# Reordering the two score units of each key tile in a relative-position attention block

## The reference

```
qh, kh, vh = heads of (q @ in_proj_weight.T + in_proj_bias);  qh = qh / sqrt(d)
scores = einsum('bhid,bhjd->bhij', qh, kh)
rel    = clip(pos[None, :] - pos[:, None], -64, 64) + 64
bias   = take_along_axis(einsum('bhid,rd->bhir', qh, rel_pe), rel)
attn   = softmax(scores + bias);  out = einsum('bhij,bhjd->bhid', attn, vh) @ out_w.T + out_b
x = layernorm(x + out)
x = layernorm(x + (gelu(x @ bw1.T + b1) @ bw2.T + b2))     # bw: alpha * sign(w)
```

## Time and profile before

| | |
|---|---|
| median of three runs | 2361.61 us (2361.12 to 2361.84) |
| profiled execution | 2361.56 us, of which the span is 2359.6 us |
| TensorE busy | 2227.5 us (94% of the span) |
| VectorE busy | 1739.1 us (74%) |
| ScalarE busy | 1573.1 us (67%) |
| GpSimd busy | 1085.8 us (46%) |
| mean granted clock of TensorE | 0.978 |

### The profile page before, as it was taken

The page is one execution under the profiler, slowest core; times in us unless marked ns, Lnnn a source line. Parts: engine busy times, 40 slices in busy tenths (PEclk is TensorE's granted clock), DMA queues, the critical chain, the costliest instruction groups (busy, mean ns, idle before and its releaser), DMA issues. The chain is left out here.

```text
span 2359.6 us, 47824 instructions
## 1 busy us (share of the span) xinstructions
PE 2227.5 (94%) x14580; PEld 1261.9 (53%) x14580; DVE 1739.1 (74%) x3447; ACT 1573.1 (67%) x2192; POOL 1085.8 (46%) x1803
## 2 busy tenths in 40 slices
PE   8996899999999999999999999999999998899997
PEld 5563444444444444444444444444444443688886
DVE  4443777777777777777777777777777772788885
ACT  3433377777777777777777777777777776466766
POOL 1001444554445544455445545454554431567663
PEclk9998599999999999999999999999999999899999
DMA  9997777777777777777777677777777752333421
GB/s 305 400 352 265 204 208 202 210 214 211 206 207 208 208 213 209 210 203 208 212 209 212 201 208 215 209 208 202 210 213 209 209 178 73 100 102 111 111 65 45
DMA packets 334570, 468.55 MB, mean 199 GB/s; under 512 B 89797, under 2 KB 262550, under 8 KB 334486
## 3 DMA queue, kind: packets, MB, share of 16 engines
q0 software_dynamic: 120960, 215.78, 33.9%
q1 hardware_dynamic: 204358, 243.32, 32.7%
q10 hardware_dynamic: 9168, 8.52, 1.1%
HBM read 244.73 MB, written 221.25 MB: 197 GB/s over the span
## 5 line engine op out<-in xcount | busy, mean ns | idle before, releaser
L933 ACT ACTIVATE probs<-weigh_ps 128x1024 f32<-128x1024 f32 x1024 | 1048.9, 1025 | 471.8 <-PE weigh_ps L1100 468.0
L985 DVE CUSTOM_DVE_ANT_1 ring_ps<-ring_ps,band_all 128x512 f32<-128x512 f32 x1008 | 681.0, 716 | 263.8 <-PE ring_ps L1061 263.6
L1061 PE MATMUL ring_ps<-keys,queries 48*128 48x512 f32 x2048 | 827.1, 468 | 40.1 <-DVE partial_max L974 14.0
L1100 PE MATMUL weigh_ps<-queries,keys 50*128 50x512 f32 (+3 forms) x2688 | 751.0, 385 | 1.3 <-ACT probs L933 0.6
L974 DVE TENSOR_REDUCE partial_max<-ring_ps 128x2 f32<-128x1024 f32 x512 | 627.7, 1226 | 112.3 <-PE ring_ps L1061 80.8
L1061 PEld LDWEIGHTS ring_ps<-keys,queries 48*128 48x128 f32 x2048 | 370.7, 187 | 524.7 <-issue 398.9
L1117 PE MATMUL sum_ps<-probs,values 128*32 128x512 f32 x4096 | 546.6, 605 | 0.1
L839 POOL COPY carried<-carried 128x252 f32<-128x252 f32 x430 | 159.3, 396 | 568.2 <-ACT carried L922 568.2
L1085 PE MATMUL weigh_ps<-ident,band_all 128*128 128x128 f32 x2048 | 363.2, 290 | 19.3 <-ACT carried L922 16.5
L1100 PEld LDWEIGHTS weigh_ps<-queries,keys 50*128 50x128 f32 x2688 | 356.3, 186 | 14.9 <-ACT probs L933 9.5
L1085 PEld LDWEIGHTS weigh_ps<-ident,band_all 128*128 128x128 f32 x2048 | 213.6, 141 | 249.9 <-ACT probs L933 104.6
(11 more groups left out here) (119 smaller groups left out, 1857.3 us busy)
## 6 DMA issues: line engine op xcount, KB each, us to landing
band_scr<-carried SPq DMA_DIRECT2D x256, 512.0 KB, 4.8
band_all<-band_scr POOLq DMA_DIRECT2D x128, 512.0 KB, 5.4
band_all<-band_scr POOLq DMA_DIRECT2D x128, 256.0 KB, 4.4
keys<-k_scr POOLq DMA_DIRECT2D x128, 240.0 KB, 8.1
k_scr<-k_parts SPq DMA_DIRECT2D x16, 1792.0 KB, 9.8
q_scr<-q_parts SPq DMA_DIRECT2D x16, 1024.0 KB, 10.4
queries<-q_scr POOLq DMA_DIRECT2D x128, 128.0 KB, 3.8
o_scr<-weighted_s SPq DMA_DIRECT2D x64, 256.0 KB, 7.6
```

Source lines behind the costliest of these rows:

```text
L933: nc.scalar.activation(probs[:, u % PROBS], weigh_ps[weigh_of["scores", at]][:], ACT.Exp).then_inc(s_pr, 1)
L985: nc.vector.tensor_tensor_reduce(out=both, in0=both, in1=bias, scale=1.0, scalar=LOWEST, op0=ALU.add, op1=ALU.max, accum_out=partial_max[: ...
L1061: nc.tensor.matmul(dst, query_rows(c, h, ROWS, tile * P, (tile + 1) * P), key_rows(c, h, ROWS, c0, c0 + 512), start=True, stop=True, tile_ ...
L1100: last = nc.tensor.matmul(weigh_ps[weigh_of["scores", at]][:, h, e0 * P:e1 * P], key_rows(c, h, QROWS, k0, k0 + P), query_rows(c, h, QROWS ...
```

## The change

Three things change together. In `weighed`, pairs 1 to 3 and 5 to 7 now take the unit without transposes first and the one with four transposes second. The band product moves from its place behind part 0 into part 1, between the two weighings. The buffers are fixed: part 0 and the band product use buffer 0, part 1 uses buffer 1. And a unit without transposes waits for its buffer at its first weighing instead of ahead of its first look.

```diff
-                return (2 * m + 1, 2 * m) if m > QT else (2 * m, 2 * m + 1)
+                return (2 * m + 1, 2 * m) if 0 < m < QT else (2 * m, 2 * m + 1)
...
+                    for what, filled, buf in ((("scores", position(step, m, 0)), step >= 0, 0),
+                                              (("band", band_index(step, m)), bands_at(step, m), 0 if step >= 0 else m % 2),
+                                              (("scores", position(step, m, 1)), step >= 0, 1)):
                         if filled:
-                            weigh_of[what], weigh_before[what] = weighs % 2, in_weigh[weighs % 2]
-                            in_weigh[weighs % 2] = what
-                        weighs += 1
+                            weigh_of[what], weigh_before[what] = buf, in_weigh[buf]
+                            in_weigh[buf] = what
...
+                def turned(u):
+                    return [t for t in range(u % 2 * QT, (u % 2 + 1) * QT) if (u // 2 - t) % NT < 2]
...
-                    wait_for(i, weigh_before["scores", at])
+                    if turned(u):
+                        wait_for(i, weigh_before["scores", at])
...
-                def weigh(c, m, part, h):
+                def weigh(i, c, m, part, h, opens):
...
-                    first = not any((n - t) % NT < 2 for t in tiles)
+                    first = not turned(u)
+                    if first and opens:
+                        wait_for(i, weigh_before["scores", at])
...
                     if step >= 0:
-                        weigh(step, m, part, 1 - first)
-                        weigh(step, m, part, first)
+                        weigh(i, step, m, part, 1 - first, True)
+                    if part == 1 and bands_at(step, m):
+                        band_product(i, band_index(step, m))
+                    if step >= 0:
+                        weigh(i, step, m, part, first, False)
...
                     products(i, step, m, 0)
-                    if bands_at(step, m):
-                        band_product(i, band_index(step, m))
                     lagging(i, step, m)
```

More of the change, by code:

```diff
@@ L668, in post_ln_block @@
             LOOK_SLOTS = (((0, 1), (2, 0)), ((1, 2), (0, 2)))
-            weighs = 0
             in_slot, in_weigh = [None] * RING, [None] * 2
@@ L687, in post_ln_block @@
                                 occupy(("look", HG * n + h), slots[h])
-                    for what, filled in ((("scores", position(step, m, 0)), step >= 0),
-                                         (("band", band_index(step, m)), bands_at(step, m)),
-                                         (("scores", position(step, m, 1)), step >= 0)):
+                    for what, filled, buf in ((("scores", position(step, m, 0)), step >= 0, 0),
+                                              (("band", band_index(step, m)), bands_at(step, m), 0 if step >= 0 else m % 2),
+                                              (("scores", position(step, m, 1)), step >= 0, 1)):
                         if filled:
-                            weigh_of[what], weigh_before[what] = weighs % 2, in_weigh[weighs % 2]
-                            in_weigh[weighs % 2] = what
-                        weighs += 1
+                            weigh_of[what], weigh_before[what] = buf, in_weigh[buf]
+                            in_weigh[buf] = what
             def cnt(i, per_step, value):
```

## The result

The changed kernel takes **2485.85 us** (median of 4 runs, 2484.74 to 2488.42) against 2361.36 us (4 runs, 2358.46 to 2361.84) for the kernel before: 1.0533 times as long, 95% interval 1.0518 to 1.0548. The forecast was 2480 us, with a range of 2425 to 2512.

What follows compares the result with a forecast made beforehand. TensorE's order, with waits between engines, was taken to bound the attention. Pairs of 5 x 3.50 + 3.44 + 3.75 + 4.12 gave +1.94 us a step, times 61.5 = 119; 2361 + 119 = 2480 us, range 2425 to 2512.

Steps and rivals of the forecast that it cites:

- Cost 1: At the seam, part 0's second look waits for VectorE to finish part 1's first look, 1.49 us; pair takes 3.50.
- Cost 2: Weighing behind the seam waits for ScalarE's band copy until 1.04 us; look possible at 1.38, covered with 0.11 to spare.
- Gain 2: Part 1 no longer needs the buffer part 0 just left, so the 0.13 us and the exponential wait go.
- Pair 0: Keeps transposes at the front, which wait for the band product's copy: 3.44 us.
- pair 4: Transposes at the front wait for the wider band copy of pair 3: 3.75 us (3.65 to 3.85).
- Pair 5: Second look waits for ScalarE's copy of the turned maxima, behind band copy and pair 4's last exponential: 4.12 us.
- The sum: All pairs of an attention step: 28.81 us against 26.87, +1.94; over 61.5 steps, 119 us.
- A: Neither wait holds at the seams, VectorE reading earlier: faster, -3.2 us a step, 2164 us; chance 0.04.
- B: Only the band copy binds at the seams: pair 3.29 us, +0.89 a step, 2416 us; chance 0.08.
- C: TensorE's clock falls in a tenth of the attention because of idling at seams: 2580 us; chance 0.05.
- D: Nothing comes of it: gains of pairs 2 and 6, waiting longest for the exponential, balance the rest, 2361 us; chance 0.03.
- the drain: Changing tiling mode drains TensorE, 0.33 us to transposes against 0.23 in the same mode; one fewer in six pairs.

Runs made afterwards that it cites:

- short reading: Changed kernel, but VectorE's band reading of the first head's look reads 128 of the 512 columns: 2423.98 us, 1.0261 times the kernel before.
- order alone: Changed kernel with only the new order of units kept; buffers in turn and band product behind part 0, as before: 2532.64 us, 1.0727 times the kernel before.
- turn's copy first: Changed kernel, but ScalarE copies the turned maxima ahead of pair 4's last exponential: 2460.19 us, 1.0413 times the kernel before.
- short copy: Changed kernel, but ScalarE copies only the last 2 of 130 columns of each narrow band product: 2468.54 us, 1.0446 times the kernel before.

## Why the prediction was right

The mechanism came out as forecast, and so did nearly every term. The lengths of the pairs, each up to its own part 1, as means of the steps between 330 and 1900 us:

| pair | 0 | 1 | 2 | 3 | 4 | 5 | 6 | 7 | step |
|---|---|---|---|---|---|---|---|---|---|
| before, us | 3.47 | 3.18 | 3.57 | 3.19 | 3.47 | 3.48 | 3.40 | 3.18 | 26.94 |
| forecast | 3.44 | 3.50 | 3.50 | 3.50 | 3.75 | 4.12 | 3.50 | 3.50 | 28.81 |
| changed | 3.46 | 3.51 | 3.51 | 3.52 | 3.77 | 4.19 | 3.52 | 3.51 | 28.97 |

Half of the loss (1.0 us) is in pairs 1, 3 and 7, a third (0.71) in pair 5 and the rest in pairs 4 and 6. Pair 2 got shorter by 0.06.

**The bank of the second look (Cost 1)** came out term by term: 3.51 against 3.50 us, look at 1.50 against 1.49, 0.43 to the sums, 1.00 and 0.58 behind them. The short reading and the order alone show that this wait is real, binding, and belongs to the order of units.

**The copy of the band product (Cost 2)** was placed right, as the wait hidden behind the other. In the seams of pairs 1, 2 and 6 the weighing begins at 1.05 in the median, forecast 1.04; in those of pairs 3 and 7, whose part 1 is split, at 1.10. ScalarE's pick-up was 0.04 in most copies, as taken from the exponentials, and 0.12 in the others; no run shows what decides between the two.

**Gain 2** came too: in the seams part 1 follows the sums by the 1.00 and 0.58 of the sums and the transposes, with no wait for an exponential. Before, it had come 1.07 behind the sums in pairs 1, 3 and 7, where 1.00 is the unhindered distance.

**Pair 0** was forecast at 3.44 (measured 3.45, part 1 from 1028.76 to 1032.21) and **pair 4** at 3.75 (measured 3.76). **Pair 5** was mis-sized by 0.08: 4.12 against 4.20. Its band product is one of those that ScalarE takes 0.12 behind the end, not 0.04, and this is carried through ScalarE's queue (the copy begins 0.69 behind part 1, forecast 0.60). The run with the turn's copy first shows that ScalarE's order does delay the turn; the first look's own wait in that pair was not in the forecast's account, though it costs nothing as long as the turn's copy ends later.

**The sum**: +1.94 us a step forecast, +2.04 measured, 119 against 124 us. The changed step is 0.16 longer than forecast, 0.07 of it in pair 5 and 0.01 to 0.02 in each other pair. The step before was 26.94 in the mean, not the 26.87 of the one step that was read, and this takes back 0.07. So a small part of the closeness is luck.

**The rivals.** A fell: in the seams the second look came at 1.50, not before 1.3. B is excluded by the short copy, and by the seams of 3.51 where it had 3.29. C did not come: the clock was 1.00 in the window. Its argument that TensorE is never idle at the low clock was wrong: the first row itself carries an idle time of 1.00 us, and TensorE was busy 48.4 of the 59 us from 236 to 295 us. D fell: pairs 0 and 2 alone kept near their length or below it, and pair 6 grew by 0.11. What pair 2 had waited for was, besides, not the exponential but the band copy behind the sums' copy, as the run that moves it shows.

On the drain, the rule of the Trainium skill's "TensorEngine Tiling (Array Packing)", Key Properties, fits the 0.33 against 0.23 of the forecast, but these rows show only that the next block comes later. That the array drains is not shown by them, and no run shows a gain from fewer changes of mode while the bank is waited for.

**What I had wrong besides**: TensorE's busy share would fall to some 88%. It stayed at 94%, because rows that had overlapped now cover the gaps between starts. The signs that did show were the releasers of single looks and the distance between starts.

## What to carry to other kernels

Two blocks of one engine that both fill a small ring of banks need something between them, as long as the reader of the oldest bank takes; moving that something to save a change of mode brings the reader's whole latency onto the path. Before such a move, add up from the producer's start to the bank's release, and compare with the distance of the starts in the new order. And when buffers are fixed to uses, the order in which the reading engine empties them is part of the same decision: the same buffers won 1.8% with the band copied first and lost 6.3% with it copied last.

## What the runs showed of the hardware

- A look of 512 columns that had to wait for a semaphore was followed by the weighted sums 0.43 us later, one that had not waited 0.33. In the trace the weight load of the first starts together with it (both at 1004.73 in the changed kernel), that of the second 0.23 us ahead of it (1002.57 and 1002.80 with the short reading).
- ScalarE's band copy began 0.04 to 0.07 us behind the product's end in 367 of 434 cases and 0.12 to 0.13 behind it in the other 67 (changed kernel, 330 to 1900 us; the ends of matmul rows are modelled by the profile). Of the exponentials of the kernel before, 875 of 932 began 0.04 behind their scores.
- TensorE's busy share stayed at 94% while the same 14580 matmuls took 124 us longer.
- VectorE's band reading of 128 columns took 0.30 us, of 512 columns 0.70; ScalarE's copy of 4 columns 0.18, of 260 columns 0.39: short forms do not shrink in proportion.
